# A Mamba and mixture-of-experts layer on one core: sixteen rounds written out on every engine in place of engine loops over pairs of rounds

## What is computed

```python
xi, res = jnp.split(x @ W_in, 2, axis=-1)
u = silu(conv1d(xi, conv_w) + conv_b)              # 256 inner channels, 4 taps
dbc = u @ W_x                                      # 8 ranks of delta, 16 of B, 16 of C
delta = softplus(dbc[..., :8] @ W_dt + b_dt)
h = exp(delta * A) * h + delta * B * u             # 16 states per channel, over time
y = (sum over states of h * C) + u * D
x = x + (y * silu(res)) @ W_out
...
scores = x @ gate_w.T                              # top 2 of 8 experts, softmax over the two
y = y + cw[:, e] * (silu(x @ w1[e].T) @ w2[e].T)   # for all 8 experts e
```

## Time and profile before

| | |
|---|---|
| median of 3 runs | 1091.44 us (1090.85 to 1091.58) |
| the profiled execution | 1092.1 us, span 1090.0 us |
| PE busy | 1040.8 us, 95% |
| DVE busy | 1017.5 us, 93% |
| POOL busy | 959.6 us, 88% |
| ACT busy | 907.1 us, 83% |
| mean granted TensorE clock | 0.978 |
| DMA | 84.12 MB, mean 77 GB/s |

### The profile page before, as it was taken

The page is one execution under the profiler, slowest core; times in us unless marked ns, Lnnn a source line. Parts: engine busy times, 40 slices in busy tenths (PEclk is TensorE's granted clock), DMA queues, the critical chain, the costliest instruction groups (busy, mean ns, idle before and its releaser), DMA issues.

```text
span 1090.0 us, 18707 instructions
## 1 busy us (share of the span) xinstructions
PE 1040.8 (95%) x6150; PEld 758.0 (70%) x6150; DVE 1017.5 (93%) x1057; ACT 907.1 (83%) x1379; POOL 959.6 (88%) x890
## 2 busy tenths in 40 slices
PE   7787789999999999999999999999999999989998
PEld 4445466677777777777776777777777776767776
DVE  5999999999999999999999999999999999999822
ACT  4987867988989999998989899899989989875533
POOL 4688886999999999999999999999999999799934
PEclk9698989999999999999999999999999999989999
DMA  5332111122040312204031311403130130320000
GB/s 202 137 127 77 71 48 79 59 108 78 1 158 28 127 59 103 82 9 173 3 126 58 126 58 40 145 0 126 58 136 39 66 109 0 137 87 11 11 8 14
DMA packets 37364, 84.12 MB, mean 77 GB/s; under 512 B 3320, under 2 KB 28208, under 8 KB 28976
## 3 DMA queue, kind: packets, MB, share of 16 engines
q1 hardware_dynamic: 36880, 83.06, 21.4%
q10 hardware_dynamic: 416, 0.30, 0.1%
HBM read 78.63 MB, written 4.72 MB: 76 GB/s over the span
## 4 chain that ended last, share of the span: by engine, by line
PE 83%; DVE 9%; issue 4%; ACT 3%; DMA 0%; POOL 0%; DVEq 0%; ACTq 0%; POOLq 0%
PE work L1829 19%; PE work L1806 18%; PE y_ps L1758 18%; PE work L1682 8%; DVE h L1258 6%; PE rows L1737 4%; PE work L1779 3%; PE work L1666 2%; PE work L1701 2%; PE rows L1829 2%; PE work L1692 2%; PE rows L1806 1%; DVE rows L1248 1%; PE y_ps L1747 1%; PE work L1727 1%
## 5 line engine op out<-in xcount | busy, mean ns | idle before, releaser
L551 POOL TENSOR_TENSOR h<-h,c_rows 128x1024 f32<-128x1024 f32 x256 | 599.9, 2364 | 53.5 <-DVE h L1258 53.2
L1258 DVE TENSOR_TENSOR_SCAN h<-dA,rows 128x1024 f32<-128x1024 f32 x256 | 579.0, 2276 | 1.1
L872 ACT ACTIVATE dA<-delta,a_neg 128x510 f32<-128x510 f32 x512 | 325.7, 707 | 7.9 <-DVE h L1258 4.4
L1248 DVE TENSOR_TENSOR rows<-du,rows 128x1024 f32<-128x1024 f32 x256 | 306.7, 1214 | 4.9 <-PE rows L1737 4.9
L1758 PEld LDWEIGHTS y_ps<-ident,h 128*128 128x128 f32 x2048 | 241.2, 144 | 62.3 <-issue 34.5
L1758 PE MATMUL y_ps<-ident,h 128*128 128x128 f32 x2048 | 270.0, 278 | 10.3 <-POOL h L551 10.3
L1829 PEld LDWEIGHTS work<-w,hid 128*128 128x128 f32 x1856 | 223.3, 193 | 34.5 <-ACT hid L906 18.9
L1806 PE MATMUL work<-x2T,w 128*128 128x512 f32 x474 | 240.2, 602 | 2.9 <-ACT u L790 2.3
L1829 PE MATMUL work<-w,hid 128*128 128x128 f32 x1856 | 229.1, 277 | 2.4 <-ACT hid L906 2.2
L906 ACT ACTIVATE hid<-work 128x512 f32<-128x512 f32 x237 | 139.3, 596 | 65.5 <-PE work L1806 63.7
L591 POOL TENSOR_TENSOR x<-x,weighted 128x512 f32<-128x512 f32 x127 | 161.9, 1274 | 19.6 <-DVE weighted L1340 19.2
(11 more groups left out here) (147 smaller groups left out, 941.7 us busy)
## 6 DMA issues: line engine op xcount, KB each, us to landing
c_rows<-c_dram SPq DMA_DIRECT2D x64, 1024.0 KB, 5.0
x_in<-in_x SPq DMA_DIRECT2D x16, 256.0 KB, 3.0
x_again<-in_x SPq DMA_DIRECT2D x16, 256.0 KB, 3.4
out<-x SPq DMA_DIRECT2D x15, 256.0 KB, 2.6
w<-in_w1T SPq DMA_DIRECT2D x1, 1024.0 KB, 4.8
w<-in_w2T SPq DMA_DIRECT2D x1, 1024.0 KB, 7.0
h<-in_conv_w SPq DMA_DIRECT2D x1, 512.0 KB, 4.9
c_dram<-bcd SPq DMA_DIRECT2D x16, 32.0 KB, 1.6
```

The source lines that it names most:

```text
L551: nc.gpsimd.tensor_tensor(at, at, c_rows[:, n, :].unsqueeze(1).broadcast_to([P, H, T]), ALU.mult).then_inc(c_used, 1)
L872: last = nc.scalar.activation(two_seqs(dA[:, n % RING, half, :])[:, :, 1:], two_seqs(delta[:, half, :])[:, :, 1:], ACT.Exp, scale=a_neg[:, ...
L1248: nc.vector.tensor_tensor(rows[:, n % 2], du[:, j.odd], rows[:, n % 2, H - 1, :].unsqueeze(1).broadcast_to([P, H, T]), ALU.mult).then_inc( ...
L1258: nc.vector.tensor_tensor_scan(h[:, n % RING].rearrange("p h t -> p (h t)"), dA[:, n % RING].rearrange("p h t -> p (h t)"), rows[:, n % 2] ...
```

## The change

`run` loses the loop: it calls the body for every round with a plain number. All five calls are changed to match, with the same first and last rounds, and nothing else is touched. Lines behind `run` move up by 7.

```diff
-    def run(eng, body, first, stages, stop):
-
-        loop_first = max(first, stages + 2)
-        pairs = (min(rounds, stop) - loop_first) // 2
-        for i in range(first, loop_first):
-            body(Round(i))
-        with eng.Fori(0, pairs) as it:
-            body(Round(loop_first, it))
-            body(Round(loop_first + 1, it))
-        for i in range(loop_first + 2 * pairs, stop):
+    def run(body, first, stop):
+
+        for i in range(first, stop):
             body(Round(i))
...
-            run(sp, round_, 7, 7, 19)
+            run(round_, 7, 19)
...
-            run(pool, round_, 5, 5, 17)
+            run(round_, 5, 17)
...
-            run(act, round_, 5, 4, 16)
+            run(round_, 5, 16)
...
-            run(dve, round_, 6, 6, 18)
+            run(round_, 6, 18)
...
-            run(pe, round_, 5, 4, 16)
+            run(round_, 5, 16)
```

## The result

The changed kernel takes 1108.72 us (median of 6 runs, 1107.85 to 1110.48), the kernel before 1091.14 (6 runs, 1090.41 to 1092.08): a ratio of 1.0162, with a 95% interval of 1.0149 to 1.0175. That is 17.6 us more. The forecast was 1108.4. The profiled execution took 1110.48 us, the longest of the six, with a span of 1108.7 us.

The account below looks back on a forecast made before the run. PE, busy 62.75 of 62.75 us in looped rounds, was taken as the bound. 10 x (0.96 + 0.47 + 0.34) + 5 x 0.14 - 1.4 = +17.0 us gave 1108.4 us, range 1103 to 1113.

Parts of the forecast that it names:

- The written-out round: Round before the looped ones, 209.42 to 274.08, hand-written on ACT: 64.66 us, 1.91 over a looped round.
- the same four waits of ACT: Written-out Silu loads all wait for the hidden projection: 1.53, 0.71, 0.64 and 0.26 us.
- the step from the profiled execution to the median: Median of the runs taken 0.7 us below the profiled execution, turning 1109.1 into 1108.4 us.
- The price of each place: Delay reaching PE per round: `hidden(four, 2, 0)` 0.96 us, `(four, 3, 0)` 0.47, `(four, 5, 0)` 0.34, `hidden(three, 0, 0)` 0.14.
- the fourth: `hidden(three, 0, 0)`: load newly held in even rounds only, already held in odd ones; 0.14 us, five times.
- The remainder put at `hidden(four, 3, 0)`: What was left of 1.91 us after the other places: 0.47 us, beside 0.38 us idle before the dt projection.
- the 0.96: `hidden(four, 2, 0)`: last projection's start to expert's start on PE, 2.06 us written out against 1.10 looped.
- 1.4 us for PE's back edges: Saving at the output projection opening a loop pass: 0.34 us per back edge, four times.
- Fetching at nothing: PE's longer written-out instruction stream costs 0; at most 3.4 us more, giving 1111.8.
- The rival on the other side: Branches are the cost, held loads cost nothing: 1090.0 to 1087.8 us; chance 0.05.
- the held loads: Silu table loads carrying the `hid_projected` wait, starting 1.28 us of loading only after PE finishes; 17 before, 56 after.
- The rival of stalls that don't add: Only some held loads reach PE, just the first place staying: 8 us more, 1099.6; chance 0.06.

Follow-up runs that it names:

- free loads: Silu table load put by hand ahead of both waits in every hidden step: changed kernel 1084.24 us (repeat 1084.2), looped kernel before 1084.83 us.
- the exchange of waits: ACT's waits on `expert_done` and `hid_projected` swapped in each hidden step: changed kernel 1084.04 us, kernel before with its loops 1104.33 us.
- the kernels of one place: Changed kernel with the Silu load put first at one place only: `hidden(., 2, 0)` 1094.49 us, `(., 3, 0)` 1101.59, `(., 5, 0)` 1105.9.

## Why the prediction was right, point by point

- **PE is full in the looped rounds, and what delays it lengthens the kernel.** Shown: 17.3 us more in ten rounds, 17.6 in the medians. Of the 1.90 us between a looped and a written-out round (62.75 and 64.65) PE idles 1.49; its busy time is 0.41 longer (63.16 for 62.75), which is within the 1% allowed for.
- **The written-out round is a sample of the changed kernel.** Shown, and this carried the forecast: 64.65 us against 64.66, with the same four waits of ACT. That the median came within 0.3 us of the forecast is more than this can claim, and luck: the six runs spread over 2.6 us, the step from the profiled execution to the median was taken as 0.7 us and was 1.8. One round in ten is an exception. From 275.14 to 340.07 it is 64.93, where the load at `hidden(four, 2, 0)` starts 0.27 us later. The same round is some 0.3 us longer wherever that load waits in written-out code, as with exchanged waits on the written-out kernel (272.39 to 335.47, 63.08 for 62.79), and not with free loads. What holds it once stays open; a fetch on ACT is not excluded.
- **The price of each place.** 0.96, 0.47, 0.34 and 0.14 us were forecast. Freed one by one they gave 1.08 (or 0.92 with the 0.16 of the expert wait taken off), 0.54 and 0.33, and 0.07 is left for the fourth, 0.12 by its rows. The remainder put at `hidden(four, 3, 0)` was too small, by 0.07. And the 0.96 was not the held load alone: 0.84 of it is, and 0.12 came with PE's own written-out form, as the run with ACT alone written out shows. The written-out round held both, so the sum did too.
- **What goes: 1.4 us for PE's back edges.** The term that was furthest off as a saving. In the run with ACT looped it came to 0.5 us, since the hand-off, 0.12 us slower with PE written out, took most of the rest. The edge itself was well sized: where no load is held the saving is 1.6. It didn't hurt the sum, which was made from whole rounds and holds both.
- **Fetching at nothing.** Right for PE: 29 packets for 6 and no gap of its own.
- **The rival on the other side** fell with the exchange of waits, which moved the cost into the loop and out of it at will. The rule of the Trainium skill that spoke for the change ("Runtime: NRT & Kernel Launch", instruction fetch mechanics) says that a taken branch stalls on a fetch where its target isn't in the window of pages at hand, and that kernels prefer full unrolling where possible. It points the right way, and the runs put a back edge at some 0.4 us of 1091. But in the kernel before, PE pays without a fetch to be seen: the queue of the earlier trace rows moved all its 6 packets before 463 us and none from there to 903, where three of PE's four back edges lie. That queue goes with PE and not with ACT: from 274 to 903 us it moved 30 packets with ACT alone looped and 7 with ACT alone written out. The rule says nothing of the held loads, which cost ten times what all the branches did.
- **The rival of stalls that don't add** fell with the kernels of one place.

## What to carry to other kernels

When a rewrite changes only how waits are expressed, look in the built order at which instruction each wait now sits on: a table load, or anything else that could run early, loses its cover if it inherits the wait of the instruction that it serves. Put such a load by hand ahead of the waits: that helped in the loop and out of it. Asking first for the wait that comes true last helped only where both counts are constants; in the loop, where a register instruction ahead of the load takes the first wait, the same order held the load. And before costing a loop's removal, search the trace for a stretch that is already written out. If it has the instructions and waits that the change will have everywhere, its length is the forecast to start from: here it held although some of the prices by places were off.

## What was not expected of the hardware

With PE written out, one hand-off from ACT takes 0.12 us longer than with register instructions and a separate wait ahead of the matmul, whether the load is free (1.22 us for 1.10) or held (2.06 for 1.94). DVE, POOL and SP changed with it, and the cause was not isolated. And the best kernels found, at 1084.0 to 1084.2 us (ratio 0.993), owe at most 1.6 us to the missing loops. The looped form with free loads, at 1084.83, is already some 7 us below the kernel before (ratio 0.9935), and only 1.3 of that lies in the ten looped rounds (628.2 for 629.5 us). The written-out round ahead of them went from 64.66 to 62.81 us, and from the last mark to the end it takes 183.6 us for 186.4. The kernel before had held loads of its own at both places, as the stall of 0.95 us at 924.02 shows.
